# PSUM in place of SBUF for the masks, temporaries and group ends of a graph network's segmented scan on one Trainium2 core

## The reference, cut to what matters

```python
msg = H[src] * norm[:, None]                       # layers 0 and 3 (layer 3 passes twice): sum
out = jax.ops.segment_sum(msg, dst, num_segments=n)
agg = jax.ops.segment_max(msg, dst, num_segments=x.shape[0])   # layer 2, four times: maximum
x_ij = h[idx_j] * Wij                              # layer 1: rows times a filter made from the edges
agg = jax.ops.segment_sum(x_ij, idx_i, num_segments=h.shape[0])
```

## Time and profile before

| what | value |
|---|---|
| median of three runs | 10543.0 us (10540.43 to 10544.05) |
| span of the profiled execution | 10630.0 us, 49732 instructions |
| POOL busy | 8032.4 us, 76% of the span |
| VectorE (DVE) busy | 4419.4 us, 42% |
| TensorE busy | 1639.5 us, 15% |
| DMA queues of software and hardware | 19.8% and 15.5% of 16 engines' span |
| one pass, from its first gather to its last | 1145.3 us (the fifth), seven of them |

### The profile page before, as it was taken

One profiled execution on the slowest core, in us unless ns is written; L12 is line 12 of the kernel. 1 busy time (PEld: TensorE's weight loads), 2 busy tenths in 40 slices (PEclk: granted clock), 3 DMA queues, 4 the chain that ended last, 5 costly groups with the idle time before them and its releaser, 6 DMA issues. The chain is left out here.

```text
span 10630.0 us, 49732 instructions
## 1 busy us (share of the span) xinstructions
PE 1639.5 (15%) x9025; PEld 1437.8 (14%) x9025; DVE 4419.4 (42%) x9272; ACT 543.8 (5%) x1417; POOL 8032.4 (76%) x7137
## 2 busy tenths in 40 slices
PE   2000048888860000100001000100001000010000
PEld 1000047777750000100001000100001000010000
DVE  4444434444443444344443444334444444444444
ACT  2000021111130000000000000000001000000000
POOL 4777768888847777677776777777777777777777
PEclk7555567777775555555555555555555555555555
DMA  5444435555532333333333333323333333333333
GB/s 190 142 142 142 145 88 77 77 74 76 77 86 91 95 95 95 99 95 95 95 97 97 95 95 95 101 93 95 95 95 98 96 95 95 95 100 95 95 95 104
DMA packets 467313, 1064.01 MB, mean 100 GB/s; under 512 B 156534, under 2 KB 276192, under 8 KB 412586
## 3 DMA queue, kind: packets, MB, share of 16 engines
q0 software_dynamic: 320736, 464.07, 19.8%
q1 hardware_dynamic: 143480, 597.45, 15.5%
q10 hardware_dynamic: 2940, 1.00, 0.0%
HBM read 517.80 MB, written 552.72 MB: 101 GB/s over the span
## 5 line engine op out<-in xcount | busy, mean ns | idle before, releaser
L991 POOL DMA_INDIRECT WORK<-table,S x5824 | 6249.0, 1073 | 2037.5 <-issue 1772.7
L1045 DVE TENSOR_TENSOR Z<-WORK,RESET 128x512 f32<-128x512 f32 x612 | 423.5, 692 | 2615.7 <-DMA WORK<-table,S 2601.8
L1210 POOL DMA_INDIRECT acc<-TOT,stage x832 | 1300.8, 1564 | 276.0 <-issue 207.6
L1090 PE MATMUL bank<-ident,WORK 128*128 128x128 f32 x7 | 3.3, 474 | 8069.6 <-DVE WORK L1074 8069.6
L1045 DVE TENSOR_TENSOR Z<-WORK,KEEP 128x512 f32<-128x512 f32 x459 | 317.6, 692 | 1958.9 <-DMA WORK<-table,S 1948.5
L1090 PEld LDWEIGHTS bank<-ident,WORK 128*128 128x128 f32 x7 | 1.3, 183 | 8071.1 <-DVE WORK L1074 8071.1
L1048 DVE TENSOR_TENSOR WORK<-WORK,Z 128x512 f32<-128x512 f32 x1071 | 741.0, 692 | 36.5
L1064 DVE TENSOR_TENSOR WORK<-WORK,Z 128x1536 f32<-128x1536 f32 (+2 forms) x448 | 633.8, 1431 | 12.4
L1059 DVE TENSOR_TENSOR Z<-WORK,S 128x1536 f32<-128x1536 f32 (+2 forms) x448 | 633.6, 1431 | 12.3
L1415 DVE SCALAR_TENSOR_TENSOR BASE<-bank,WEIGHT,BASE 128x128 f32<-128x128 f32 x832 | 234.2, 344 | 839.8 <-PE bank L1285 772.3
L1053 DVE SCALAR_TENSOR_TENSOR WORK<-WORK,S 128x128 f32<-128x128 f32 x1428 | 502.5, 352 | 50.9
(11 more groups left out here) (247 smaller groups left out, 2663.4 us busy)
## 6 DMA issues: line engine op xcount, KB each, us to landing
run_rows<-WORK SPq DMA_DIRECT2D x357, 1024.0 KB, 4.1
WORK<-table,S POOLq DMA_INDIRECT x5824
fill_rows<-BASE SPq DMA_DIRECT2D x52, 1024.0 KB, 6.8
WORK<-fill_rows SPq DMA_DIRECT2D x104, 512.0 KB
table<-TF SPq DMA_DIRECT2D x56, 384.0 KB
WORK<-carry_rows SPq DMA_DIRECT2D x49, 384.0 KB
acc<-TOT,stage POOLq DMA_INDIRECT x832
acc<-Z SPq DMA_DIRECT2D x12, 1024.0 KB
```

The source lines that it names most:

```text
L991: pool.indirect_dma_start(RING_T[:, b * WIDE + k, :], None, table, table_row(table, INDEX[:, t:t + 1]))\
L1045: step(dve.tensor_tensor(TMP[:, 0:groups, 0, :], rows[:, :, j - 1, :], mask(keep[:, :, j], groups, 0), op0))
L1210: pool.indirect_dma_start(acc_dram[a], bass.IndirectOffsetOnAxis(stage[:, h, j % HALF:j % HALF + 1].bitcast(u32), 0), TOT[:, j // QUAD % 2 ...
```

## The change

Four banks' worth of tensors become one PSUM tensor of eight banks of 512 columns each. At the start of each pass VectorE copies the mask of all 832 columns (`scale`, that is RESET or KEEP) into `STEP` (banks 0 and 1) and `PREFIX` into `FROM` (banks 6 and 7). `TMP` moves to banks 2 to 4. The last column of each group of four no longer goes back to WORK by line 1048 but into `ENDS` (bank 5), from where line 1053 takes it. That line's own factor, one number per partition, stays in SBUF. Counts, shapes and the order of the scan's operations are the same. The one-column scan of the last 16 columns, the gathers and the stores are not changed.

```diff
-        TMP = Z[:, 0:3 * GROUPS * F].rearrange("p (g j f) -> p g j f", g=GROUPS, j=3)
-        banks = [ctx.enter_context(nc.psum_tensor(f"bank{i}", [P, 1024], f32)) for i in range(4)]
+        banks = ctx.enter_context(nc.psum_tensor("bank", [P, 8 * 512], f32))
+        STEP = banks[:, 0:T]
+        TMP = banks[:, 2 * 512:5 * 512].rearrange("p (g j f) -> p g j f", g=GROUPS, j=3)
+        ENDS = banks[:, 5 * 512:6 * 512].rearrange("p (g f) -> p g f", g=GROUPS)
+        FROM = banks[:, 6 * 512:6 * 512 + T]
...
-            return banks[i // 2][:, i % 2 * 512:(i % 2 + n) * 512]
+            return banks[:, i * 512:(i + n) * 512]
...
                 if masks is not None:
                     prefix_masks(dve, st, masks)
+                st.did(dve.tensor_copy(STEP, scale[:]))
+                st.then(dve.tensor_copy(FROM, PREFIX))
...
-                    keep = scale[:, t0:t0 + FOUR * groups].rearrange("p (g j) -> p g j", j=FOUR)
-                    prefix = PREFIX[:, t0:t0 + FOUR * groups].rearrange("p (g j) -> p g j", j=FOUR)
+                    keep = STEP[:, t0:t0 + FOUR * groups].rearrange("p (g j) -> p g j", j=FOUR)
+                    prefix = FROM[:, t0:t0 + FOUR * groups].rearrange("p (g j) -> p g j", j=FOUR)
...
-                        step(dve.tensor_tensor(rows[:, :, j, :], rows[:, :, j, :], TMP[:, 0:groups, 0, :], op1))
+                        step(dve.tensor_tensor(ENDS[:, 0:groups, :] if j == FOUR - 1 else rows[:, :, j, :],
+                                               rows[:, :, j, :], TMP[:, 0:groups, 0, :], op1))
...
+                        k = t0 + FOUR * g + FOUR - 1
                         step(dve.scalar_tensor_tensor(RING_T[:, last, :], RING_T[:, (last - FOUR) % SPAN, :],
-                                                      prefix[:, g, FOUR - 1:FOUR], RING_T[:, last, :], op0, op1))
+                                                      PREFIX[:, k:k + 1], ENDS[:, g, :], op0, op1))
```

## The result

The changed kernel takes **9791.6 us** (median of 4 runs, 9787.0 to 9793.9) against 10543.2 us before: a ratio of 0.9287, 95% interval 0.9274 to 0.9300. The forecast was 9795 us. The profiled execution of the changed kernel has a span of 9785.2 us.

A forecast was written before the change was run, and what follows sets the result against it. The prediction took POOL's one-after-another issue of 832 gathers per pass as the bound, some held by VectorE operations. Its terms -748 + 0 + 0 + 0 us, from the 10543 us median, gave 9795 us, range 9780 to 9925.

The forecast's parts named there:

- POOL's gathers set the pass: In each pass, POOL issuing 832 gathers one after another sets the length; VectorE, stores and transfers run in its shadow.
- The holds cost 751 us, 748 of them under lines 1045 to 1064: Gathers starting during VectorE operations wait for their end: 751.1 us over 0.944 us per gather, 748 us freed by the change.
- One SBUF input ends the hold: Lines 1045, 1048, 1059, 1064: with one SBUF input every gather takes 0.944 us, passes 1038 us instead of 1145, -748 us.
- its twelve gathers: Line 841's gathers in the updates, beginning within operations like lines 1177 and 1169, all 940 to 945 ns: evidence of no hold.
- PSUM costs VectorE nothing: Reading masks and temporaries from PSUM and writing temporaries there: taken as 0, though no row shows VectorE writing to PSUM.
- Line 1053 has nothing to gain: Line 1053 held no gather with two SBUF inputs already, so 0; the rival that it holds in its new place, chance 0.05.
- The upper end of 126 us: Line 1053 holding one gather per chunk for at most one operation, 357 x 0.352 us; as rival 9921 us, chance 0.05.
- The copies are free: Two 832-column mask copies at each pass's start, 1.02 us each, 14 in all: 0 on the path, at most 14 us.
- The median as the base: The 748 us saving is taken from the median of 10543 us, as what is freed is POOL's time in both.
- the 87 us between the span and the median of before: The old kernel's profiled span of 10630.0 us stood 87 us (0.8%) above the median of its three runs.

## Why the prediction was right

- *POOL's gathers set the pass.* Right: the passes shrank by what the gathers' sum did, 107.7 and 106.9 us in the two windows, and VectorE's chain could be made 1.8 times as long for 12 us.
- *The holds cost 751 us, 748 of them under lines 1045 to 1064.* Right: 5499.0 us of gathers remain where 5500 were expected. Passes of 1038.4 us against 1038 forecast.
- *One SBUF input ends the hold.* Right, and shown from both sides by the temporaries alone and the masks alone. The prediction's own evidence was thinner than it looked: of its twelve gathers (940 to 946 ns, not 945), eight began where two SBUF inputs hold a gather in these runs; the other four began 2 ns into the operation or in its last 140 ns, where none is held. That a held gather leaves the operation as long as ever is right, but a gather that comes just after the operation's start lengthens it. The inference of the Trainium skill's page "SBUF — State Buffer" ("Who interferes with whom"), that `tensor_tensor` doesn't hold a DMA issued by POOL, isn't borne out for these indirect gathers: with the masks in SBUF, `tensor_tensor` at line 1066 held one to 2.46 us. The Trainium skill's rule on two SBUF inputs, in the same section, is.
- *PSUM costs VectorE nothing.* Right within 5 ns: 696 ns for a 128x512 operation that writes PSUM, 687 for one that reads it and writes SBUF, 692 before. This was the one price without a row, so the 0 was a choice and not a finding; it came out so.
- *Line 1053 has nothing to gain.* Right in size, with the reason incomplete and some luck. Two SBUF inputs at 128 columns do hold, in a part of their time only, and the gathers of before happened to come outside it. The upper end of 126 us assumed a full operation per chunk; the ends in the ring gave 7.6.
- *The copies are free.* Right, 1.03 us each and no hold; the copy into PSUM shows it at 357 times.
- *The median as the base.* It held: the changed kernel's span stands within 7 us of its median, and the passes' gain in the two profiles is the medians'. That the 87 us between the span and the median of before lay outside the passes is inferred from this.

## What to carry to other kernels

Where POOL's indirect DMAs set the pace, look at the spread of their durations before counting them: a minimum well under the mean, with long ones that all end the same time after a VectorE operation, is time that VectorE takes from POOL while it isn't itself the bound. Moving one of two SBUF inputs to PSUM gave it back here without making VectorE slower. Move both halves of a pair: with one half moved, 18% or 42% of the gain was left here, since a gather freed from one operation ran into the next. Keep fast copies inside SBUF out of such a loop, or send them to PSUM.

## What the runs showed that I had not expected

- A hold doesn't cover the whole operation. For 352 ns over 128x128 elements it caught gathers that started about 100 to 200 ns after it, 45 in the run with the ends in the ring and none in the kernel before, whose gathers began 310 ns in. Longer operations leave the last 140 ns or so free too: with the masks in SBUF, 319 gathers began in the last 147 ns of line 1050's 699 and none was held, as the one 680 ns in here:

```profile
6333.43 0.70 DVE L1050 TENSOR_TENSOR bank<-WORK,RESET 128x512 f32<-128x512 f32 x1
6334.11 0.94 POOL L994 DMA_INDIRECT WORK<-table,S  x1 [0.30 <-issue]
```

A held gather ends some 0.82 us after the operation and a free one takes 0.944, so I estimate that the part which waits comes about 0.13 us after a gather's start; a gather that gets there after the operation's end needn't wait. What in the gather waits no run shows. So a short operation with two SBUF inputs costs little, and how much depends on the phase.

- Returning half of the operations to SBUF returned 80% of the holds' cost (599 of 751 us) in one way and 57% (427 of 751) in the other.
- In the runs with the temporaries in SBUF and with the copy inside SBUF, gathers that nothing held took 947 ns in place of 944, some 17 us in all. The other runs stayed at 944. Why isn't settled.
